# Layers' weighted values in 64x32 tiles of the array: each product of 64 value columns becomes two of 32

## The chip, the cores and the metric

The kernel is one program on one core of a Trainium2 chip. The time is the device time of one execution in microseconds (us). Lower is better.

## The reference, cut to what matters

The model has two blocks over x of shape (4, 512, 128). The first block has a test-time-training layer and then a stack of six transformer layers. The second has an attention with relative positions and a mixture of experts. The change touches only the six layers. Each layer projects x to queries, keys and values of 16 heads of width 64, normalizes and rotates q and k, and attends locally: each window of 32 tokens sees itself and the 32 tokens before it.

```python
DIM, DEPTH, HEADS, DIM_HEAD, WINDOW = 128, 6, 16, 64, 32
def local_attention(q, k, v):              # q, k, v: b h n d
    bq, bk, bv = (t.reshape(b, h, nw, w, d) for t in (q, k, v))
    bk2, bv2 = look(bk), look(bv)          # the window before and the own one: 2*w keys
    sim = jnp.einsum('bhwie,bhwje->bhwij', bq, bk2) * QK_SCALE
    sim = jnp.where(mask, -jnp.finfo(sim.dtype).max, sim)
    attn = jax.nn.softmax(sim, -1)
    out = jnp.einsum('bhwij,bhwje->bhwie', attn, bv2)
    return out.reshape(b, h, n, d)
for i in range(DEPTH):
    x = attn_layer(shift_tokens(x), Wqkv[i], ...) + x
    x = ffn_layer(shift_tokens(x), ln_g[i], ...) + x
```

The last `einsum` is the step that is changed: for each head and window, 32 rows of 64 weights times 64 rows of 64 values.

## The kernel before

All data is float32. The program has four phases that end in a meeting of all engines: test-time training, the transformer layers, the relative attention, the experts. The layers take the stretch from about 188 to 1830 us of the profiled execution.

**Tiling of the layers.** A unit is one layer for one of the 4 batch rows, so there are 24 units, u = 4 * layer + batch. A unit has 4 tiles of 128 tokens, and a tile has two parts (h = 0 and 1, eight heads each): 192 parts in all, counted m. A part goes through: scores (`PE`), a scaling copy and the row maximum (`DVE`), exponentials (`ACT`), reciprocals (`DVE`), scaling (`POOL`), a transpose of the weights (L1216, `PE`), a copy of the transposed weights to `pT` (L1360, `ACT`), the product with the values (L1226, `PE`), and a copy of the result to `oT` (L1365, `ACT`). After the second part of a tile the result goes through the output projection (L1234, `PE`).

**Order.** No planner runs. `rounds()` writes out, once for all engines, a list of (kind, number, step), and each engine runs through it and issues what it has at each step. A part starts every 4 rounds, and `PART_AT` gives its steps: score 0, turn 5, weigh 6, o_copy 8, mix 9. So in the order of TensorE the weighing of one part stands between the scores of later parts, and around both stand the next unit's projections (L1109 to L1111, 512 columns each), the sums of squares (L1139) and the feed-forward network of an earlier unit (L1159 to L1185). TensorE runs everything in that order. It waits by semaphores for what other engines must have ready, for instance `pt_kept` before the weighing.

**The scores, L1208.** Per part a loop over 4 groups, 2 halves, 4 blocks of 32 tokens and 2 heads gives 64 calls of `matmul`. Each uses 32 rows and 32 columns of the array and streams 64 columns. The trace holds 128 weight loads and 128 matmuls for it: a float32 product is two pairs of instructions.

**The weighing, L1226.** Per part a loop over a (2), blk (4), o (2) and f (2) gives 32 calls, 64 pairs of instructions in the trace. f picks the head of a pair, which lies in partitions 64f to 64f + 63 of `pT` and of `v_win`. The 64 value columns are the stationary operand and the 32 tokens of a window the streamed one. The result goes to partitions `to` to `to + 63` of bank 2 + o, with `to` = 64 * ((f + o) % 2), so that four calls in a row use the four 64x64 tiles of the array.

**Buffers around it.** `v_win` is read from the second buffer of two and is filled by DMAs from SP's queue. Before a new one is filled, SP waits for `weighted` of two tiles earlier. ACT's copy to `oT` waits for `weighted` of the same part. The transposes of the next part wait for this copy.

Of the kernel before, what the change touches and what calls it, by code (L numbers as in the profile page):

```python
# [16 lines left out]
P = 128  # L17
# [7 lines left out]
DEPTH, HEADS, DH, WIN = 6, 16, 64, 32  # L25
# [685 lines left out]
GROUPS_TF, HALF_D = 4, DH // 2  # L711
# [167 lines left out]
def ring_take(c, t, *user):  # L879
    k = t.ring[user]  # L880
    if k >= 2:
        c.PE.wait_ge(*ring_freed(t, *t.ring_users[k - 2]))
    return ring_bank(c, t, *user)
# [198 lines left out]
def transformer_tensor(c, t):  # L1082
    PE, psum = c.PE, c.psum
    norm_center(c, t, 0)
    table_tensor(c, t, 0)
    norm_sums(c, t, 0)
    for n in range(1, len(TABLES)):
        table_tensor(c, t, n)
    norm_spread(c, t, 0)
    for b in range(1, B):  # L1090
        norm_center(c, t, b)
    for b in range(1, B):
        norm_sums(c, t, b)
    PE.wait_ge(*t.once.all())
    PE.wait_ge(*t.prepared.on(0))
    PE.wait_ge(*t.tab_kept.all())
    for now in rounds():
        for kind, n, s in now:
            if kind == "spread":
                norm_spread(c, t, n)  # L1100
            elif kind == "part":
                part_tensor(c, t, n, s)
            elif kind == "unit":
                unit_tensor(c, t, n, s)
# [84 lines left out]
def part_tensor(c, t, m, s):  # L1189
    PE, psum, (n, h) = c.PE, c.psum, divmod(m, 2)  # L1190
    u, i = divmod(n, TPB)
    q, k, v = t.q[u % 2], t.k[u % 2], t.v[n % 2]
    if s == PART_AT["score"]:
        PE.wait_ge(*t.k_scaled.on((u, GROUPS_TF - 1)))
        PE.wait_ge(*t.made.on((u, 2 * GROUPS_TF - 1)))
        if m:
            PE.wait_ge(*t.scores_kept.on(m - 1))
        mask = t.maskb[:, 0 if i == 0 else 1, :].unsqueeze(1).to_broadcast([P, GROUPS_TF, 2 * WIN])
        for x in range(2):
            PE.e.matmul(psum[:, x, 0:GROUPS_TF * 2 * WIN].rearrange("p (g k) -> p g k", g=GROUPS_TF), c.identb[:, :], mask, start=True, stop=False)  # L1200
        for g in range(GROUPS_TF):
            for half in range(2):
                for blk in range(TPB):
                    tok, out = i * P + blk * WIN, slice(g * 2 * WIN, (g + 1) * 2 * WIN)
                    for f in range(2):
                        j = 2 * h + f
                        rows = slice(HALF_D * j, HALF_D * (j + 1))
                        last = PE.e.matmul(psum[WIN * blk:WIN * (blk + 1), f, out], q[rows, g, half, tok:tok + WIN], k[rows, g, half, tok:tok + 2 * WIN],  # L1208
                                           start=False, stop=(half == 1 and g == GROUPS_TF - 1))
        last.then_inc(*t.scored.by(m))  # L1210
    if s == PART_AT["turn"]:
        PE.wait_ge(*t.p_scaled.on(m))
        if m:
            PE.wait_ge(*t.o_kept.on(m - 1))
        for g in range(GROUPS_TF):
            last = PE.e.transpose(psum[:, 2, g * P:(g + 1) * P], t.p[h][:, g, :, :].rearrange("p f k -> p (f k)"), c.ident[:, :])  # L1216
        last.then_inc(*t.turned.by(m))
    if s == PART_AT["weigh"]:
        PE.wait_ge(*t.pt_kept.on(m))
        PE.wait_ge(*t.v_in[n % 2].on((n, 9 if i else 7)))  # L1220
        for a in range(2):
            for blk in range(TPB):
                for o in range(2):
                    for f in range(2):
                        rows, to, at = slice(DH * f, DH * f + DH), (f + o) % 2 * DH, a * P + blk * WIN
                        last = PE.e.matmul(psum[to:to + DH, 2 + o, at:at + WIN], v[rows, blk, 2 * (2 * a + o) + h, :],  # L1226
                                           t.pt[h][rows, 2 * a + o, blk * WIN:(blk + 1) * WIN], start=True, stop=True)
        last.then_inc(*t.weighted.by(m))
    if s == PART_AT["mix"] and h == 1:
        PE.wait_ge(*t.o_kept.on(m))  # L1230
        PE.wait_ge(*t.wo_in.on((u // B, 7)))
        ps = ring_take(c, t, "part", m, "mix")
        for e in range(PAIRS):
            last = PE.e.matmul(ps[:, 0:P], t.wo[:, e, :], t.ot[e % 2][:, e // 2, :], start=(e == 0), stop=(e == PAIRS - 1))  # L1234
        last.then_inc(*t.mixed.by(n))
# [1256 lines left out]
```

## Time and profile before

| | us |
|---|---|
| median of 3 runs | 2531.78 |
| lowest and highest | 2521.78, 2538.67 |
| span of the profiled execution | 2515.4 |
| TensorE matmul busy in it | 2362.9 (94%), 53,677 instructions |
| TensorE weight loads busy | 1738.9 (69%), 53,677 instructions |
| VectorE, ScalarE, GpSimd busy | 1744.7, 1598.6, 1463.1 |

Matmuls and weight loads are listed apart, since a load runs beside the matmuls ahead of it. Matmuls are pipelined: the next one starts before the last one has ended, so a group's busy time is the time covered by at least one of its matmuls, and its mean is the length of a single one with its latency. "issue" as a releaser means that the engine waited for nothing that the profile shows, that is, for its own instructions.

### The profile page before, as it was taken

The numbers are of one execution on the slowest core, as the hardware profiler recorded it, in microseconds if no ns is written. First come the engines' busy times: TensorE is split into PE (matmuls) and PEld (weight loads), VectorE is DVE, ScalarE is ACT, GpSimd is POOL, SyncE is SP. The second block draws the span as 40 slices with busy tenths as digits, with TensorE's granted clock in tenths as the row PEclk, the third lists the DMA queues.
The fourth block names the chain that finished last, engine by engine and source line by source line (L and its number), as shares of the span: only waits on it lengthen the run. The fifth ranks groups of instructions, "written<-read, shape, count | busy, mean of one in ns | idle before, by whom it ended". The sixth has DMA issues, their size and how long they took to land.

```text
span 2515.4 us, 122084 instructions
## 1 busy us (share of the span) xinstructions
PE 2362.9 (94%) x53677; PEld 1738.9 (69%) x53677; DVE 1744.7 (69%) x3537; ACT 1598.6 (64%) x5036; POOL 1463.1 (58%) x1408
## 2 busy tenths in 40 slices
PE   9958999999999999999999999999878999999967
PEld 8836777777777777777777777777645666666657
DVE  4477888888878888878787888887335555555534
ACT  3226777777777787777777877777625444545422
POOL 1166667656666667666666677665117656566307
PEclk9979999999999999999999999999979999999978
DMA  4013333333333334333333343333216222222136
GB/s 91 15 33 86 85 78 96 95 80 85 93 88 94 81 83 103 92 83 81 88 95 85 79 97 82 84 92 84 57 22 185 48 48 48 48 48 48 30 95 250
DMA packets 230210, 204.62 MB, mean 81 GB/s; under 512 B 133687, under 2 KB 155464, under 8 KB 229552
## 3 DMA queue, kind: packets, MB, share of 16 engines
q1 hardware_dynamic: 225296, 190.91, 30.6%
q8 instruction: 422, 6.91, 1.2%
q0 software_dynamic: 2208, 5.58, 0.6%
q14 instruction: 108, 0.88, 0.1%
q10 hardware_dynamic: 2176, 0.33, 0.1%
HBM read 86.05 MB, written 15.70 MB: 40 GB/s over the span
## 4 chain that ended last, share of the span: by engine, by line
PE 72%; DVE 17%; issue 4%; SPq 2%; ACT 2%; DMA 1%; POOL 1%; POOLq 0%; ACTq 0%; DVEq 0%
PE psum L1208 8%; PE psum L1226 6%; PE psum L1955 5%; PE psum L1234 5%; PE psum L1109 5%; PE psum L1934 5%; PE psum L1940 4%; PE psum L1111 4%; PE psum L1110 3%; DVE kT L1443 3%; PE psum L1989 3%; PE psum L1979 3%; DVE rotated L1418 3%; PE psum L1185 2%; PE psum L1216 2%
## 5 line engine op out<-in xcount | busy, mean ns | idle before, releaser
L1354 ACT ACTIVATE p<-p,stat 128x64 f32<-128x64 f32 x1536 | 512.5, 336 | 40.1 <-DVE stat L1490 38.0
L1573 POOL TENSOR_TENSOR p<-p,inverse 128x512 f32<-128x512 f32 x192 | 200.2, 1043 | 465.9 <-DVE inverse L1493 464.9
L1208 PE MATMUL psum<-kT,qT 32*32 32x64 f32 x24576 | 306.7, 223 | 30.3 <-issue 29.1
L2088 DVE TENSOR_REDUCE largest<-psum 128x1 f32<-128x512 f32 x256 | 165.0, 686 | 228.0 <-PE psum L1940 228.0
L1208 PEld LDWEIGHTS psum<-kT,qT 32*32 32x32 f32 x24576 | 264.0, 103 | 82.2 <-issue 81.1
L1354 ACT ACTIVATION_READ_ACCUMULATOR p<-p,stat 128x1 f32 x1536 | 288.6, 188 | 0.0
L1418 DVE SCALAR_TENSOR_TENSOR rotated<-psum,scales,rotary 128x512 f32<-128x512 f32 x384 | 271.1, 742 | 24.3 <-ACT sq L1290 24.2
L1552 POOL TENSOR_TENSOR sq<-sq 128x512 f32<-128x512 f32 x192 | 245.1, 1276 | 42.4 <-ACT sq L1290 42.1
L1290 ACT ACTIVATE sq<-psum 128x512 f32<-128x512 f32 x384 | 212.8, 581 | 63.3 <-PE psum L1139 45.9
L1226 PEld LDWEIGHTS psum<-pT,v_win 64*64 64x64 f32 x12288 | 197.3, 135 | 47.6 <-issue 40.6
L1109 PE MATMUL psum<-xs,wqkv_high 128*128 128x512 f32 x384 | 204.9, 534 | 24.3 <-DVE rotated L1418 24.3
L2010 ACT ACTIVATE w_by_key<-psum 128x512 f32<-128x512 f32 x128 | 76.4, 597 | 230.5 <-PE psum L1955 230.5
L1226 PE MATMUL psum<-pT,v_win 64*64 64x32 f32 x12288 | 218.6, 221 | 1.5 <-ACT pT L1360 1.5
L1234 PEld LDWEIGHTS psum<-oT,wo 128*128 128x128 f32 x1536 | 188.0, 196 | 37.0 <-issue 28.0
L1234 PE MATMUL psum<-oT,wo 128*128 128x128 f32 x1536 | 198.9, 283 | 7.5 <-issue 4.2
L1360 ACT ACTIVATE pT<-psum 128x512 f32<-128x512 f32 x192 | 114.3, 596 | 135.7 <-PE psum L1216 135.5
L1303 ACT ACTIVATE v_tok<-psum 128x512 f32<-128x512 f32 x192 | 113.8, 593 | 96.5 <-PE psum L1111 78.7
L2100 POOL TENSOR_TENSOR q_by_head<-q_heads,mask_head 64x256 fp32r<-64x256 f32 x252 | 156.8, 622 | 15.4
L1559 POOL TENSOR_TENSOR qT<-qT,rotated 128x512 f32<-128x512 f32 x96 | 165.7, 1726 | 0.0
L2056 ACT ACTIVATE weights<-psum,largest 128x512 f32<-128x512 f32 x256 | 161.3, 687 | 3.6 <-DVE largest L2088 3.6
L1443 DVE TENSOR_TENSOR kT<-kT,rnorm_wide 128x1024 f32<-128x1024 f32 x96 | 155.7, 1622 | 5.4 <-DMA rnorm_wide<-rnorms 5.3
L1111 PE MATMUL psum<-xs,wqkv_high 128*128 128x512 f32 x384 | 155.0, 404 | 0.0
(352 smaller groups left out, 5448.6 us busy)
## 6 DMA issues: line engine op xcount, KB each, us to landing
v_win<-v_tok SPq DMA_DIRECT2D x576, 128.0 KB
rnorm_wide<-rnorms SPq DMA_DIRECT2D x384, 64.0 KB
v_win<-v_tok SPq DMA_DIRECT2D x336, 64.0 KB
q_rows<-q_rows_all SPq DMA_DIRECT2D x32, 512.0 KB, 4.6
tile_weights<-expert_table SPq DMA_DIRECT2D x23, 512.0 KB, 6.1
wqkv<-L_ffn_Wqkv SPq DMA_DIRECT2D x96, 64.0 KB, 2.4
rel_values<-sq SPq DMA_DIRECT2D x60, 64.0 KB, 2.2
wo<-L_ffn_Wo SPq DMA_DIRECT2D x48, 64.0 KB
```

The source lines that it names most:

```text
L1109: PE.e.matmul(out, w[0], x[1], start=True, stop=False)
L1111: return PE.e.matmul(out, w[0], x[0], start=False, stop=True)
L1208: last = PE.e.matmul(psum[WIN * blk:WIN * (blk + 1), f, out], q[rows, g, half, tok:tok + WIN], k[rows, g, half, tok:tok + 2 * WIN], start= ...
L1226: last = PE.e.matmul(psum[to:to + DH, 2 + o, at:at + WIN], v[rows, blk, 2 * (2 * a + o) + h, :], t.pt[h][rows, 2 * a + o, blk * WIN:(blk + ...
L1234: last = PE.e.matmul(ps[:, 0:P], t.wo[:, e, :], t.ot[e % 2][:, e // 2, :], start=(e == 0), stop=(e == PAIRS - 1))
L1290: A.e.activation(t.sq[half][:, :], c.psum[:, 4 + half, :], ACT.Square).then_inc(*t.squared.by((u, (p, half))))
L1354: last = A.e.activation(p, p, ACT.Exp, bias=t.stat[:, h, 2 * g + f:2 * g + f + 1], accum_out=t.sum[:, h, g, f:f + 1])
L1418: last = V.e.scalar_tensor_tensor(out=rot[x], in0=psum[:, 4 + half, :], scalar=scale, in1=table, op0=ALU.mult, op1=ALU.mult)
L1443: V.e.tensor_tensor(k, k, t.wide[g % 2][:, :].unsqueeze(1).to_broadcast([P, 2, S]), ALU.mult).then_inc(*t.k_scaled.by((u, g)))
L1552: G.e.tensor_tensor(t.sq[0][:, :], t.sq[0][:, :], t.sq[1][:, :], ALU.add).then_inc(*t.squares.by((u, p)))
L1559: G.e.tensor_tensor(second, second, t.turned_by[1][:, :], ALU.add).then_inc(*t.made.by((u, p)))
L1573: G.e.tensor_tensor(p, p, t.inv[:, h, :, :].unsqueeze(3).to_broadcast([P, GROUPS_TF, 2, 2 * WIN]), ALU.mult).then_inc(*t.p_scaled.by(m))
```

## The change

In the weighing of a part the loop over the 64 value columns is split in two halves of 32 (`HALF_D` is 32). A new loop over d = 0 and 32 stands outside the loops over o and f. Each call now loads 64 rows by 32 value columns, writes 32 partitions of the result beginning at `to + d`, and streams the same 32 columns of `pT`. So eight calls in a row use eight tiles of 64x32. The number of calls per part goes from 32 to 64. What is computed, the banks, the semaphores and everything else stay the same.

```diff
         for a in range(2):
             for blk in range(TPB):
-                for o in range(2):
-                    for f in range(2):
-                        rows, to, at = slice(DH * f, DH * f + DH), (f + o) % 2 * DH, a * P + blk * WIN
-                        last = PE.e.matmul(psum[to:to + DH, 2 + o, at:at + WIN], v[rows, blk, 2 * (2 * a + o) + h, :],
-                                           t.pt[h][rows, 2 * a + o, blk * WIN:(blk + 1) * WIN], start=True, stop=True)
+                for d in range(0, DH, HALF_D):
+                    for o in range(2):
+                        for f in range(2):
+                            rows, to, at = slice(DH * f, DH * f + DH), (f + o) % 2 * DH + d, a * P + blk * WIN
+                            last = PE.e.matmul(psum[to:to + HALF_D, 2 + o, at:at + WIN], v[rows, blk, 2 * (2 * a + o) + h, d:d + HALF_D],
+                                               t.pt[h][rows, 2 * a + o, blk * WIN:(blk + 1) * WIN], start=True, stop=True)
         last.then_inc(*t.weighted.by(m))
```

## Rows read from the trace of the kernel before

**Rows 1.** The page: busy time and share of each engine, and the chain.

```profile
PE 2362.9 (94%) x53677; PEld 1738.9 (69%) x53677; DVE 1744.7 (69%) x3537; ACT 1598.6 (64%) x5036; POOL 1463.1 (58%) x1408
...
PE 72%; DVE 17%; issue 4%; SPq 2%; ACT 2%; DMA 1%; POOL 1%; POOLq 0%; ACTq 0%; DVEq 0%
```

**Rows 2.** Windows of 300 us and the layers' whole: busy us (instructions), clock, DMA.

```profile
600.00:900.00 300.00, 291.26 (x7922) 1.00 0.37 90
188.00:1830.00 1642.00, 1583.30 (x43483) 0.99 0.35 86
```

**Rows 3.** Groups by line and form: count, busy us, mean ns, idle before.

```profile
L1208 PE MATMUL psum<-kT,qT 32*32 32x64 f32 x24576 | 306.7, 223 | 30.3 <-issue 29.1
L1226 PE MATMUL psum<-pT,v_win 64*64 64x32 f32 x12288 | 218.6, 221 | 1.5 <-ACT pT L1360 1.5
L1109 PE MATMUL psum<-xs,wqkv_high 128*128 128x512 f32 x384 | 204.9, 534 | 24.3 <-DVE rotated L1418 24.3
...
L1216 PE MATMUL psum<-ident,p 128*128 128x128 f32 x768 | 117.5, 276 | 17.6 <-POOL p L1573 14.5 <-ACT oT L1365 2.6
```

**Rows 4.** The same view for the weight loads.

```profile
L1208 PEld LDWEIGHTS psum<-kT,qT 32*32 32x32 f32 x24576 | 264.0, 103 | 82.2 <-issue 81.1
L1226 PEld LDWEIGHTS psum<-pT,v_win 64*64 64x64 f32 x12288 | 197.3, 135 | 47.6 <-issue 40.6 <-ACT pT L1360 6.9
```

**Rows 5.** Timeline of the matmuls: start us, length us, what, count.

```profile
607.53 0.43 PE L1139 MATMUL psum<-sq,onehot 128*32 128x128 f32 x8
607.88 1.14 PE L1226 MATMUL psum<-pT,v_win 64*64 64x32 f32 x64
608.95 0.50 PE L1109 MATMUL psum<-wqkv_low,xs 128*128 128x512 f32 x1
...
610.77 1.48 PE L1208 MATMUL psum<-kT,qT 32*32 32x64 f32 x128
```

**Rows 6.** Timeline of the loads in the first 0.2 us of a scores' stage.

```profile
627.29 0.29 PEld L1208 LDWEIGHTS psum<-kT,qT 32*32 32x32 f32 x32 [0.21 <-issue]
```

**Rows 7.** The page: the queue that brings TensorE's instructions.

```profile
q8 instruction: 422, 6.91, 1.2%
```

**Rows 8.** Timeline of the loads: two scores' stages that are interrupted.

```profile
616.75 1.22 PEld L1208 LDWEIGHTS psum<-kT,qT 32*32 32x32 f32 x116 [0.21 <-issue]
618.92 0.17 PEld L1208 LDWEIGHTS psum<-kT,qT 32*32 32x32 f32 x12 [0.95 <-issue]
...
650.84 0.94 PEld L1208 LDWEIGHTS psum<-kT,qT 32*32 32x32 f32 x89 [0.21 <-issue]
652.08 0.48 PEld L1208 LDWEIGHTS psum<-kT,qT 32*32 32x32 f32 x39 [0.30 <-issue]
```

**Rows 9.** Windows between such interruptions: us, loads busy (count), clock, DMA.

```profile
618.91:652.07 33.16, 24.92 (x889) 1.00 0.38 101
652.07:686.94 34.87, 24.18 (x889) 1.00 0.34 84
...
704.66:738.88 34.22, 24.12 (x888) 1.00 0.40 89
615.38:618.91 3.53, 2.03 (x137) 1.00 0.29 64
648.98:652.07 3.09, 2.22 (x142) 1.00 0.32 70
```

**Rows 10.** Who waited for whom: us in total, times, longest.

```profile
PEld psum L1208 <- issue: 81.1, 259, 2.0
```

**Rows 11.** The line of the weighing: first and last start.

```profile
L1226 PE MATMUL psum<-pT,v_win x12288: 186/219/313, 197.1 to 1829.4; 64*64 64x32 f32 x199
```

## The prediction

> **What bounds the kernel now.** I read the page first. TensorE's matmuls cover 94% of the span and no other engine more than 69%; in the chain of work that ended last, 72% is TensorE's [rows 1]. Next the windows: in the layers, where the change lies, TensorE is busy for 1583 of 1642 us, and for 291 of 300 us in their middle, at the full granted clock of 2.4 GHz [rows 2]. So time added to TensorE's order in the layers shows almost whole in the end, and time saved there too, unless it falls where TensorE waits for others. There are few such waits: 24.3 us for the rotations, 17.6 us before the transposes, 1.5 us before the weighing [rows 3]. Last I read the groups by line and the timeline, since a busy share does not say what holds the engine. A 94% busy engine may be computing, loading weights, or be short of instructions.
>
> **What the weighing costs now.** 192 parts with 64 pairs (load and matmul) each take 218.6 + 1.5 = 220.1 us, 1.146 us a part [rows 3]; the timeline has 1.14 us for a typical one, with the next stage 1.07 us after its start [rows 5]. A matmul's own length, 0.22 us, is latency that the next ones overlap. So 64 starts lie within 1.14 - 0.22 = 0.92 us, 14.6 ns apart. The matmuls stream only 32 columns, whereas a load of 64 columns lasts 135 ns and one of 32 columns 103 ns [rows 4]. I read this stage as held by its loads: each of four tiles takes its next load only every four pairs.
>
> **What the change does to the array.** Every load has half the columns and eight tiles instead of four take turns. If loads bind, a tile needs less time per load and twice as many tiles work at once, so the array could do twice the pairs in less than the present time. The saving can't be more than the stage has, and it isn't there for the taking: the instructions double, from 128 to 256 a part, 12,288 pairs or 24,576 instructions in all. The question is how fast TensorE gets its instructions.
>
> **The price of a pair in 128 pairs.** The scores are the nearest row: 128 pairs a part, eight tiles in turn. They take 306.7 + 30.3 = 337.0 us, 1.755 us a part [rows 3]. Three facts in them:
> - The first 32 pairs go fast: 32 loads in 0.29 us, less 0.10 us for the length of the last, 31 gaps of 6.1 ns [rows 6]. I take them as instructions that had been queued while the long matmuls ahead ran.
> - A scores' stage without interruption takes 1.48 us in all [rows 5], so (1.48 - 0.22)/127 = 9.9 ns a pair. Beyond the first 32 the pairs come slower, though the array shows at the start that it can take them at 6.1 ns. So in the rest they come at the pace of supply, about 11 ns.
> - Some stages are interrupted by "issue" for 0.3 to 0.95 us [rows 8]. Between two such places there are 889, 889 and 888 loads [rows 9], some 7 x 127. The instruction queue moved 6.91 MB in 422 packets [rows 7]: 16 KB each, and 6.91 MB over 2 x 53,677 instructions is 64 bytes, so a packet is 256 instructions, 128 pairs less a few semaphore instructions. The interruptions stand at multiples of a packet. The packets ahead of two of them lasted 3.53 and 3.09 us [rows 9]. So a packet that is used up in under about 3 to 3.5 us has to wait for the next.
>
> The weighing now runs at 14.6 ns a pair, slower than the supply, and shows no such wait. With 128 pairs at 32 columns it becomes a stage like the scores.
>
> **The sum, on the profiled execution's 2515.4 us.**
> - Lower end of the added time: every weighing costs as an uninterrupted scores' stage: 1.48 - 1.14 = 0.34 us x 192 = 65 us.
> - As an average scores' stage: 1.755 - 1.146 = 0.61 us x 192 = 117 us. Of these, (1.755 - 1.48) x 192 = 53 us are interruptions.
> - Interruptions become more frequent. Parts follow each other every (1829.4 - 197.1)/191 = 8.55 us [rows 11]. The layers hold 43,483/192 = 226 pairs a part [rows 2], 1.77 packets, 4.8 us each. After: 290 pairs, 2.27 packets in about 9.2 us, 4.05 us each, near the 3.1 to 3.5 us at which a packet is late, and now both scores and weighing use one up within 1.5 us. Twice 53 us are at stake (scores and weighing); I take half more, +53 us. The bounds are 0 and twice as much more, +106 us, with a further 30 us for longer waits at each.
> - Taken up by waits of TensorE that exist now (24.3 + 17.6 us [rows 3] and smaller ones): -15 us, between 0 and -40.
>
> Sum: 117 + 53 - 15 = 155 us, so 2670 us for a profiled execution. The median of the runs lies 16 us above the profiled span (2531.78 against 2515.4), so I forecast 2687 us, 6% slower. ACT's copy to `oT` comes 0.3 to 0.6 us later in each part and with it the next transposes; these are two rounds off and TensorE is the one that is late for them, so I add nothing. If the copy had no such room, 192 x 0.3 us would be added, within the range. SP's refill of `v_win`, which waits for the weighing of two tiles earlier, moves by the same fraction of a microsecond in a distance of two tiles (17 us): nothing.
>
> The Trainium skill speaks against the interruptions: its page "Runtime: NRT & Kernel Launch", section "Instruction fetch mechanics", has TensorE's instructions brought in blocks of 16 KB by a queue of their own while earlier ones run, so that crossing a block is mostly hidden. The trace agrees on the block and not on the hiding. By that page alone the sum would be the 65 us of the lower end at most. Its page "TensorE: Matmul & The Clock Gate", in the section "Wait — 56ns, not 53.3ns?", puts the least distance of two matmuls at about 25 ns; by that a stage of 128 pairs would take over 3 us, and the scores' 9.9 ns here rule it out.
>
> **The rivals.**
> - *Supply keeps up, the stage gets shorter (the other sign).* If all 128 pairs came at the 6.1 ns of the first 32, a stage would take 127 x 6.1 ns + 0.22 us = 0.99 us against 1.14: -0.15 x 192 = -28 us, 2504 us. It decides from below (1.14 - 0.22)/127 = 7.2 ns a pair. For it: the loads are smaller than the scores' and the streamed columns are half, so if the 11 ns later in the scores' stage were the array's doing and not the supply's, the weighing would escape it. Against it: the same tiles and forms ran at 6.1 ns just before. Chance 0.05.
> - *No change.* The stage gets to about 7.2 ns a pair, or waits elsewhere in the layers take up all: they are some 40 us against 65 at least. 2531 us. Chance 0.05.
> - *Supply floor alone.* Packets come in time, as for scores without interruption: 65 - 15 = 50 us, 2582 us. For it: many scores' stages have no interruption, 259 waits for issue in all against 192 that each stage has at its start [rows 10]. Against it: the packets of the weighing come on top. Chance 0.16.
> - *The supply of packets becomes the bound.* Every scores' and weighing stage waits for its packet. 117 + 106 + 30 = 253 us and more, 2785 us. It decides when a packet takes 4 us or more, since the 2.27 packets a part then fill the part's whole time. Chance 0.12.
> - *As forecast*, interruptions in both stages, 2600 to 2770 us. Chance 0.62.
>
> **Range and chances.** The range 2580 to 2785 holds the forecast and the better part of its two neighbours. Measurements of this kernel tell a difference from about 1%. Slower by over 1%: 0.90 (the last three cases); within 1%: 0.05; faster by over 1%: 0.05.
>
> **What would show it.** In the profile after: TensorE has 53,677 + 12,288 = 65,965 matmuls; the instruction queue some 96 packets more (24,576/256); the weighing's line shows 24,576 matmuls of form 64*32, with loads near 103 ns. If the forecast is right, a weighing stage has 1.4 us or more in the timeline with 128 pairs, its group gets idle time by "issue", the busy time and idle time of L1226 together go from 220 to 340 us or more, and the scores' line, which isn't touched, also gains idle time by issue over its 30.3 us. If the supply floor alone holds, the scores' line stays at 337 us. If the rival with the other sign is right, the weighing's stage is 1.0 us long and without issue waits. I am wrong on the cause if the stage is longer with evenly spaced pairs from the very first, since then the array and not the supply limits a 64x32 tile.

## The result, and the profile after

| | before | after |
|---|---|---|
| median | 2531.4 us (4 runs) | 2809.84 us (4 runs) |
| span of the profiled execution | 2515.4 us | 2803.6 us |
| mean granted clock over the span | 0.971 | 0.938 |

The changed kernel is 11% slower: the ratio is 1.110, with a 95% interval of 1.107 to 1.114. The profiled spans differ by 288 us. The forecast was 155 us more for the profiled execution and 2687 us for the median, with 2785 us as the upper end of the range.

The page of the changed kernel answers [rows 1] and [rows 7]:

```profile
PE 2502.6 (89%) x65965; PEld 1841.9 (66%) x65965; DVE 1741.3 (62%) x3537; ACT 1603.8 (57%) x5036; POOL 1432.5 (51%) x1408
...
q8 instruction: 518, 8.49, 1.3%
...
PE 86%; issue 8%; DVE 2%; POOL 1%; DMA 1%; ACT 1%; another core or an unknown queue 0%; ACTq 0%; POOLq 0%; SPq 0%; DVEq 0%
```

TensorE has the 12,288 matmuls more that were expected, and its instruction queue the 96 packets more. Yet TensorE is busy for only 89% instead of 94% of a longer span, and in the chain "issue", time without any other releaser, goes from 4% to 8%. So TensorE is more on the path that sets the end, and stands idle more. The groups by line (out<-in, form, count | busy us, mean ns of one | idle us before, releaser) answer [rows 3] and [rows 4]. L1227 is the weighing, L1235 the output projection:

```profile
L1208 PE MATMUL psum<-kT,qT 32*32 32x64 f32 x24576 | 330.9, 229 | 107.4 <-issue 106.4
L1227 PE MATMUL psum<-pT,v_win 64*32 64x32 f32 x24576 | 262.8, 201 | 58.9 <-issue 57.2 <-ACT pT L1361 1.4
L1235 PE MATMUL psum<-oT,wo 128*128 128x128 f32 x1536 | 234.0, 314 | 19.2 <-issue 18.4 <-ACT oT L1366 0.7
...
L1208 PEld LDWEIGHTS psum<-kT,qT 32*32 32x32 f32 x24576 | 273.0, 106 | 169.3 <-issue 168.2
L1227 PEld LDWEIGHTS psum<-pT,v_win 64*32 64x32 f32 x24576 | 234.2, 105 | 112.9 <-issue 104.4 <-ACT pT L1361 7.4
```

Busy and idle time of each line, added up:

| line | before | after | difference |
|---|---|---|---|
| weighing | 220.1 | 321.7 | +101.6 us |
| scores (not touched) | 337.0 | 438.3 | +101.3 us |
| output projection (not touched; 198.9 + 7.5 before) | 206.4 | 253.2 | +46.8 us |
| the rest of 288.2 | | | +38.5 us |

Only about a third of the loss lies in the line that was changed. Of the last row, 15.5 us lie behind the layers, in phases that the change doesn't touch: from the last start of the weighing to the end of the span it is 686.0 us before (2515.4 less 1829.4 [rows 11]) and 701.5 us after (2803.6 less 2102.1). In the traces of the experiments below it takes between 680 us (with half of the change) and 700 us (with kernels that have none of it), so these 15.5 us can't be put down to the change. The layers themselves lost 273 us. The timeline of TensorE in one stretch shows how the loss comes about (start us, length us, what, count, idle before):

```profile
682.40 1.22 PE L1227 MATMUL psum<-pT,v_win 64*32 64x32 f32 x120
685.51 0.33 PE L1227 MATMUL psum<-pT,v_win 64*32 64x32 f32 x8 [1.89 <-issue]
...
687.80 2.05 PE L1208 MATMUL psum<-kT,qT 32*32 32x64 f32 x128
...
691.65 3.62 PE L1235 MATMUL psum<-oT,wo 128*128 128x128 f32 x16
...
697.64 1.29 PE L1227 MATMUL psum<-pT,v_win 64*32 64x32 f32 x128
```

And the windows around it (us; busy us and count of PE, PEld, DVE, ACT, POOL; granted clock, DMA share, GB/s):

```profile
683.50:685.00 1.50, 0.12 (x14) 0.01 (x1) 1.33 (x6) 1.49 (x8) 0.00 (x0) 1.00 0.00 0
685.00:695.20 10.20, 9.69 (x160) 7.40 (x160) 5.03 (x12) 2.17 (x4) 4.80 (x4) 0.50 0.43 106
695.20:700.00 4.80, 4.80 (x157) 3.97 (x156) 3.64 (x17) 3.87 (x19) 0.65 (x1) 1.00 0.37 83
```

The weighing stops after 120 of its 128 matmuls for 1.89 us. Then the granted clock is 0.50 (the lower level, 1.2 GHz) for 10.2 us, in which the scores take 2.05 us without any interruption (1.48 us in [rows 5]) and the output projection 3.62 us. A weighing without interruption takes 1.29 us. Its loads in the first 0.2 us:

```profile
697.64 0.26 PEld L1227 LDWEIGHTS psum<-pT,v_win 64*32 64x32 f32 x33 [0.20 <-issue]
```

The first 33 pairs come (0.26 - 0.10)/32 = 5 ns apart, against 8.6 ns over the whole stage. So the pairs are not evenly spaced from the very first, which the prediction had named as the sign that the array and not the supply limits a 64x32 tile.

The trace's record of the transfers on TensorE's instruction queue ties the waits to the packets. In the layers of the changed kernel, TensorE's matmuls waited for issue 192 times for more than 0.3 us, and each of these waits ends 2.2 to 3.0 us after the start of the latest packet's transfer. The closest two packets start 3.26 us apart, and on average one starts every 4.4 us.

### The profile page after: what moved, and what is told of

It is laid out like the page before. It is cut to its first block, busy times and chain, and to the rows that moved or that the text cites. A ratio compares the mean times of both kernels' runs of the same rounds, so it can differ in the third digit from the quotient of the medians.

```text
span 2803.6 us, 146660 instructions
## 1 busy us (share of the span) xinstructions
PE 2502.6 (89%) x65965; PEld 1841.9 (66%) x65965; DVE 1741.3 (62%) x3537; ACT 1603.8 (57%) x5036; POOL 1432.5 (51%) x1408
## 4 chain that ended last, share of the span: by engine, by line
PE 86%; issue 8%; DVE 2%; POOL 1%; DMA 1%; ACT 1%; another core or an unknown queue 0%; ACTq 0%; POOLq 0%; SPq 0%; DVEq 0%
PE psum L1208 11%; PE psum L1227 9%; PE psum L1235 8%; PE psum L1109 7%; PE psum L1111 5%; PE psum L1110 5%; PE psum L1956 5%; PE psum L1935 4%; PE psum L1216 3%; PE psum L1941 3%; PE psum L1177 3%; PE psum L1990 2%; PE psum L1139 2%; PE psum L1180 2%; PE psum L1980 2%
## 5 line engine op out<-in xcount | busy, mean ns | idle before, releaser
L1208 PE MATMUL psum<-kT,qT 32*32 32x64 f32 x24576 | 330.9, 229 | 107.4 <-issue 106.4
L1208 PEld LDWEIGHTS psum<-kT,qT 32*32 32x32 f32 x24576 | 273.0, 106 | 169.3 <-issue 168.2
L1227 PE MATMUL psum<-pT,v_win 64*32 64x32 f32 x24576 | 262.8, 201 | 58.9 <-issue 57.2
L1227 PEld LDWEIGHTS psum<-pT,v_win 64*32 64x32 f32 x24576 | 234.2, 105 | 112.9 <-issue 104.4
L1235 PEld LDWEIGHTS psum<-oT,wo 128*128 128x128 f32 x1536 | 223.5, 226 | 58.5 <-issue 53.4
L1235 PE MATMUL psum<-oT,wo 128*128 128x128 f32 x1536 | 234.0, 314 | 19.2 <-issue 18.4
L1109 PE MATMUL psum<-xs,wqkv_high 128*128 128x512 f32 x384 | 207.9, 541 | 24.0 <-DVE rotated L1419 24.0
L1486 DVE TENSOR_TENSOR p<-psum,rnorm_tok 128x512 f32<-128x512 f32 x192 | 131.7, 686 | 62.3 <-PE psum L1208 54.2
L1419 DVE SCALAR_TENSOR_TENSOR kT<-psum,scales,rotary 128x512 f32<-128x512 f32 x192 | 142.9, 744 | 43.9 <-PE psum L1208 25.4
L1559 POOL TENSOR_TENSOR kT<-kT,rotated 128x512 f32<-128x512 f32 x96 | 122.8, 1279 | 71.4 <-DVE kT L1419 70.9
```

The source lines that it names most:

```text
L1109: PE.e.matmul(out, w[0], x[1], start=True, stop=False)
L1227: last = PE.e.matmul(psum[to:to + HALF_D, 2 + o, at:at + WIN], v[rows, blk, 2 * (2 * a + o) + h, d:d + HALF_D], t.pt[h][rows, 2 * a + o, b ...
L1419: last = V.e.scalar_tensor_tensor(out=rot[x], in0=psum[:, 4 + half, :], scalar=scale, in1=table, op0=ALU.mult, op1=ALU.mult)
```

## The experiments

Two theories stood against each other in the expectations. *Supply*: TensorE gets its instructions in packets of 256; a packet used up too early leaves it waiting, and these waits are the loss. *Tile*: the 64x32 form is slow by itself. Beside them stood the clock, as a cost of its own or not.

**The new tiles without more instructions**

```diff
-                for d in range(0, DH, HALF_D):
+                for d in (range(0, DH, HALF_D) if m == 0 else (blk % 2 * HALF_D,)):
```

> The weighing uses 64x32 tiles as in the changed kernel, but only one of the two halves of 32 value columns is computed (the lower in even blocks of 32 tokens, the upper in odd ones; the first part has both): 64 pairs of instructions a part, as many as before, and half of the values is left out. Supply theory (the time goes where TensorE waits for packets of 256 instructions): the new form costs nothing by itself; the weighing takes under 0.8 us a part, the scores' line stays near its 337 us busy and idle, and the whole is 2460 to 2500 us, faster than before. Tile theory (64x32 tiles or their changes of mode are slow by themselves): the weighing's pairs cost as in the changed kernel (307 us / 24,576 = 12.5 ns) and what it does to the scores (some 100 us more) stays, so 2570 to 2600 us.

2514.1 us against 2530.33, ratio 0.994 (0.989 to 0.999). The lines by form of this kernel:

```profile
L1208 PE MATMUL psum<-kT,qT 32*32 32x64 f32 x24576 | 308.9, 223 | 45.7 <-issue 45.0
L1227 PE MATMUL psum<-pT,v_win 64*32 64x32 f32 x12352 | 148.4, 200 | 3.6 <-issue 2.0 <-ACT pT L1361 1.6
```

The form isn't slow: 64 pairs cost 152.0/192 = 0.79 us a part, against 1.146 us in 64x64 tiles. That speaks against the tile theory. But the whole became faster by 16 us, far less than the 68 us that the line lost, and the 2460 to 2500 us that the supply theory had given were missed. The scores took back 18 us (354.6 against 337.0, where the expectation had them unchanged). A likely reason, which no run isolates, is that the parts follow each other faster and the packets with them. In the waits of TensorE, those for ACT's copy to `oT` and for the softmax's scaling are now 8.1 and 24.3 us (3.2 and 14.5 before).

**The old tiles with as many instructions**

```diff
+def tiny_products(c, n, bank):
+    for k in range(n):
+        to = k % 4 * HALF_D
+        c.PE.e.matmul(c.psum[to:to + HALF_D, bank, k:k + 1], c.ident[:, 0:HALF_D], c.ident[:, 0:1], start=True, stop=True)
...
         PE.wait_ge(*t.v_in[n % 2].on((n, 9 if i else 7)))
+        tiny_products(c, 32, 3)
         for a in range(2):
```

> The kernel before with its 64x64 tiles, and ahead of each weighing 32 products of one streamed column (128 rows, 32 columns of the array), whose results are overwritten: the instruction count of the changed kernel in other forms. Supply theory: the scores, which are not touched, lose as in the changed kernel (their line goes from 337 to 420 us and more, with the growth in idle time by issue), the output projection too, and the whole is 2740 to 2810 us. Tile theory: the additional pairs cost only themselves, 64 x 6 to 8 ns x 192 = 75 to 100 us, so 2605 to 2630 us, and the scores stay at 337 us.

2784.03 us, ratio 1.099 (1.095 to 1.103). Its lines:

```profile
L1215 PE MATMUL psum<-kT,qT 32*32 32x64 f32 x24576 | 322.7, 228 | 60.4 <-issue 58.9
L1234 PE MATMUL psum<-pT,v_win 64*64 64x32 f32 x12288 | 231.5, 221 | 36.9 <-issue 36.9
...
L1193 PE MATMUL psum<-ident 128*32 128x1 f32 x12288 | 145.7, 172 | 2.3 <-ACT pT L1368 1.4 <-issue 0.5
```

The whole is within 1% of the changed kernel, without one 64x32 tile in the weighing. It lies in the range of the supply theory partly by luck: the tiny products themselves cost 148 us, where I had worked out 75 to 100 us. The rest stands in lines that were not touched, 124 us together: scores +46 us (383.1), weighing +48 us (268.4), output projection +30 us (217.0 + 19.2 = 236.2). This is the part that shows what more instructions do to their neighbours. The scores' loss is half of what the changed kernel has, so that part of the expectation was missed.

**The same additional instructions, spread**

```diff
+        tiny_products(c, 16, 4 + at)
         three_products(PE, psum[:, 4 + at, :], w, xs).then_inc(*t.projected.by((u, (p, at))))
```

> The same number of tiny products, but 16 ahead of each of the 16 projections of a unit instead of 32 ahead of each weighing: as many instructions per part, away from the dense stages. If only the density in a burst mattered (scores and weighing back to back), the scores would stay near 337 us and the whole near 2531 + 75 to 100 us = 2605 to 2630 us. If the number of packets in the time matters as well, since each has to be used up later than some 3.4 us after the last, the scores still lose 40 to 80 us and the whole is 2680 to 2760 us, below the run with the same products at the weighing.

2757.04 us, ratio 1.089 (1.085 to 1.092).

```profile
L1216 PE MATMUL psum<-kT,qT 32*32 32x64 f32 x24576 | 309.9, 224 | 55.2 <-issue 54.2
L1234 PE MATMUL psum<-pT,v_win 64*64 64x32 f32 x12288 | 220.4, 221 | 2.1 <-ACT pT L1368 1.5 <-issue 0.4
L1194 PE MATMUL psum<-ident 128*32 128x1 f32 x12288 | 175.2, 174 | 24.3 <-DVE rotated L1426 16.7 <-issue 7.1
```

Here the products take 199.5 us with the waits for `rotated` that now fall on them. The harm to others is smaller: scores +28 us, weighing +2 us. So where the instructions stand matters. The total is in the expected range, but the scores' loss is below the 40 to 80 us that I had given. The total is only 27 us lower than with the products at the weighing, because 384 short stages cost more by themselves than 192.

**Nothing but instructions.** Behind the kernel's last work:

```diff
+            for k in range(2048):
+                rows, to = slice(DH * (k % 2), DH * (k % 2) + DH), k // 2 % 4 * HALF_D
+                c.PE.e.matmul(c.psum[to:to + HALF_D, k % 2, 0:1], c.ident[rows, 0:HALF_D], c.ident[rows, 0:1], start=True, stop=True)
```

> The kernel before, and behind its last work a stream of 2048 products of one column in 64x32 tiles: 4096 pairs, 8192 instructions, 32 packets, with nothing else running. Supply theory: a packet comes every 3.4 to 3.9 us whatever is in it, so 27 to 30 ns a pair, 109 to 125 us for the stream. If the supply were what the uninterrupted scores' stage shows (9.9 ns a pair), 41 us; if it kept the pace of the first 32 pairs (6.1 ns), 25 us.

2644.12 us, 114 us more; this kernel was timed once. Timeline of the loads, and a window over 29 such groups:

```profile
2533.25 1.26 PEld L158 LDWEIGHTS psum<-ident 64*32 64x32 f32 x128 [2.02 <-issue]
2536.72 1.26 PEld L158 LDWEIGHTS psum<-ident 64*32 64x32 f32 x128 [2.21 <-issue]
2540.19 1.26 PEld L158 LDWEIGHTS psum<-ident 64*32 64x32 f32 x128 [2.21 <-issue]
...
2533.20:2638.30 105.10, 36.67 (x3712) 0.50 0.02 5
```

This shows the supply by itself. TensorE takes just 128 pairs in 1.26 us and then has nothing for 2.0 to 2.8 us, again and again: 105.1/29 = 3.62 us for each packet of 256 instructions. The DMA share is 0.02, so the packet's time isn't contention with other transfers. The granted clock is 0.50 in this window, but the 3.3 us between the closest packets of the layers, where the clock is mostly 1.00, is about the same as here (3.33 us), so the supply's pace isn't an effect of the lower clock. Within a packet the pairs come (1.26 - 0.10)/127 = 9.1 ns apart.

**The change where the scores are short, and its base.** Both kernels take half of the scores' products:

```diff
-            for half in range(2):
+            for half in range(1):
...
-                                           start=False, stop=(half == 1 and g == GROUPS_TF - 1))
+                                           start=False, stop=(g == GROUPS_TF - 1))
```

> The kernel before with half of the products of the scores: only the first 32 of each head's 64 dimensions are multiplied, so the scores are not complete, and a part has 32 products there (64 pairs) instead of 64. It is the base for the next run. Supply theory: without a stage of 128 pairs hardly any stage waits for a packet; the scores' line falls from 337 us to 130 to 170 us, idle time by issue near 0, and the whole is 2330 to 2370 us.

> The changed kernel with the same halved scores: the layers' instruction count of the kernel before, the dense stage of 128 pairs now at the weighing. Supply theory: the harm of the change depends on what stands beside it, so here it costs only 90 to 150 us over the other run with halved scores (2440 to 2500 us) instead of the 278 us that it costs in full; the weighing's line keeps 230 us and more busy with 20 to 50 us idle by issue, the scores stay short. Tile theory (the 64x32 form has its price by itself): the same 278 us on top, 2610 to 2650 us.

Base: 2506.41 us, ratio 0.992 (0.989 to 0.995). With the change: 2535.19 us, ratio 1.003 (1.001 to 1.005). So here the change costs 29 us, not 278, and also far less than the 90 to 150 us of the supply theory's expectation. First the lines of the base, then the lines of the other:

```profile
L1234 PE MATMUL psum<-oT,wo 128*128 128x128 f32 x1536 | 203.1, 287 | 47.9 <-ACT oT L1365 45.5
L1216 PE MATMUL psum<-ident,p 128*128 128x128 f32 x768 | 122.2, 283 | 61.1 <-POOL p L1573 47.5 <-ACT oT L1365 12.4
...
L1226 PE MATMUL psum<-pT,v_win 64*64 64x32 f32 x12288 | 219.6, 221 | 2.6 <-ACT pT L1360 1.9
L1208 PE MATMUL psum<-kT,qT 32*32 32x64 f32 x12288 | 165.1, 223 | 0.0
```

```profile
L1227 PE MATMUL psum<-pT,v_win 64*32 64x32 f32 x24576 | 267.3, 201 | 40.2 <-issue 37.1 <-ACT pT L1361 1.9
L1208 PE MATMUL psum<-kT,qT 32*32 32x64 f32 x12288 | 181.6, 223 | 49.3 <-issue 49.0
...
L1235 PE MATMUL psum<-oT,wo 128*128 128x128 f32 x1536 | 199.6, 284 | 16.4 <-ACT oT L1366 13.9 <-issue 2.1
L1216 PE MATMUL psum<-ident,p 128*128 128x128 f32 x768 | 117.2, 275 | 13.3 <-POOL p L1574 10.9 <-ACT oT L1366 2.2
```

I was wrong on the base by 136 us and more: 172 us less in the scores made the kernel only 22 us faster. TensorE now waits for the softmax (47.5 us) and for the copy to `oT` (45.5 us). So another chain ends nearly as late as TensorE's work, and what is taken from TensorE brings little.

The same waits make the 29 us too small as a price of the change. Its weighing loses 85 us (222.2 to 307.5, with 40 us idle), for 102 us in the full kernel. The scores, which were to stay short, lose 66 us (165.1 to 230.9) for 101 us there. Together that is some 50 us less harm. The output projection, which lost 47 us there, waits for issue for only 2.1 us here, and the mean granted clock is no lower with the change (0.966 against 0.961 over the profiled spans). On the other side, waits of the base were filled: the line of the output projection is 35 us and that of the transposes 53 us shorter than in the base. So the lines shown put some 100 us of the difference between 278 and 29 us down to harm that didn't occur, and some 80 us to room that the base has; the rest isn't settled. A fixed price of 278 us, as the tile theory has it, would leave some 200 us even with that room. The price depends on what stands beside the change, as supply says.

**Half of the change.** The 32-column form only in parts with h = 0:

```diff
-                for d in range(0, DH, HALF_D):
+                wide = DH if h else HALF_D
+                for d in range(0, DH, wide):
...
-                            last = PE.e.matmul(psum[to:to + HALF_D, 2 + o, at:at + WIN], v[rows, blk, 2 * (2 * a + o) + h, d:d + HALF_D],
+                            last = PE.e.matmul(psum[to:to + wide, 2 + o, at:at + WIN], v[rows, blk, 2 * (2 * a + o) + h, d:d + wide],
```

> The change in every second part only (h = 0 as in the changed kernel, h = 1 with 64x64 tiles as before): 2.02 packets of 256 instructions a part instead of 2.27 or 1.77. A price per changed part (tile form) gives just half of the 278 us, 2665 to 2675 us. Supply theory with a threshold (a packet hurts only when used up in under some 3.4 us): it rises faster at the end than at the start, so the first half of the change costs less than the second: 90 to 130 us, 2620 to 2660 us.

2609.77 us against 2518.07 beside it, ratio 1.037 (1.034 to 1.040). Half of the change costs 3.7%, a third of the 11% of the whole. A fixed price per changed part would give 5.5%. The lines tell where the difference arises:

```profile
L1208 PE MATMUL psum<-kT,qT 32*32 32x64 f32 x24576 | 315.7, 224 | 54.9 <-issue 54.1
L1228 PE MATMUL psum<-pT,v_win 64*32 64x32 f32 x12288 | 136.4, 201 | 27.6 <-issue 26.6 <-ACT pT L1362 0.7
L1228 PE MATMUL psum<-pT,v_win 64*64 64x32 f32 x6144 | 111.1, 222 | 0.7 <-ACT pT L1362 0.7
```

The weighing itself loses 56 us (275.8 against 220.1), about half of the 102 us of the full change. The scores lose only 34 us (370.6) of 101 us. So it is the harm to the neighbours that grows faster at the end, as a threshold has it.

**The scores in two pieces**, a long group of matmuls between them, before and after the change (`rest_tensor` issues the second piece and is called behind each of the long groups):

```diff
...
+        scores(range(GROUPS_TF // 2))
+        t.rest = lambda: scores(range(GROUPS_TF // 2, GROUPS_TF)).then_inc(*t.scored.by(m))
```

> The kernel before, complete, with the scores of a part issued in two pieces of 64 pairs and the next long group of matmuls (a projection, an output projection or a part of the feed-forward network) between them. Supply theory: each piece is mostly in TensorE's queue when it begins and packets are used up more evenly: the scores' line loses 30 to 80 us of its 337 us, and the whole is 2460 to 2510 us if the later scores don't make TensorE wait for the softmax. If instead the order only shifts work, the time stays within 1% of 2531 us; if the delay of the scores hits the transposes, more than 20 us are added.

> The changed kernel with the scores in two pieces in the same way, the weighing in one. Supply theory: as many packets a part (2.27), but spread better, so 2700 to 2770 us against 2810 us, with less idle time by issue in the scores' line than the 107 us of the changed kernel. Tile theory: no difference from 2810 us beyond 1%.

Before with two pieces: 2586.4 us, ratio 1.023 (1.021 to 1.026), slower instead of faster. After with two pieces: 2807.48 us, ratio 1.111 (1.107 to 1.115), no difference from the changed kernel, which is what the tile theory had said; the supply theory had said 2700 to 2770 us. Line, timeline and two waits of the first:

```profile
L1225 PE MATMUL psum<-kT,qT 32*32 32x64 f32 x24576 | 331.4, 222 | 0.2
...
646.74 0.85 PE L1225 MATMUL psum<-kT,qT 32*32 32x64 f32 x64
648.42 0.85 PE L1225 MATMUL psum<-kT,qT 32*32 32x64 f32 x64
...
PE psum L1255 <- ACT oT L1387: 24.5, 50, 1.6
PE psum L1149 <- DVE z L1519: 22.5, 21, 1.1
```

The interruptions did go: 30.3 us of idle time before, 0.2 now. But two pieces take 2 x 0.85 = 1.70 us, one undisturbed stage 1.48, and the later scores make TensorE wait for the copy and for the sum in z. So supply can be smoothed by order, and it didn't pay. After the change the scores' line still has 59.1 us idle by issue (106.4 in the changed kernel). Between the two kernels with pieces the change costs 221 us (2807.48 less 2586.4), not 278, so the smoother order does soften the change, by about as much as the pieces themselves cost. Why these two cancel so closely isn't settled, and by its total this run doesn't speak for supply.

**More work for the array per instruction**

```diff
+                if a == 1 and blk % 2 == 0:
+                    PE.e.matmul(psum[:, 3, 256:512]..., c.identb[:, :], t.maskb[:, 1, :]..., start=True, stop=True)
```

> The changed kernel with two pairs more in each weighing: a bf16 matmul of 128x128 by 256 columns that keeps the array busy for about 0.11 us each and whose result nobody reads. It asks whether the fall of the granted clock (TensorE is at the lower of its two levels for some 200 us of the layers, against some 20 us before) is a cost of its own that more array work per instruction takes back. If so, the time at the lower level falls to 100 us or less, the output projection's line (234 us, 199 us before) falls towards 210 us, and the total rises by less than the 2 x 0.11 x 192 = 42 us that the matmuls take. If the clock only follows the waits, nothing of it changes and the total rises by 40 to 90 us.

2786.78 us against 2518.07 beside it, ratio 1.107 (1.104 to 1.111), where the changed kernel has 1.110 (1.107 to 1.114): the 384 additional matmuls cost nothing that can be measured. Its output projection, its filling matmuls, and the windows of the layers for this kernel:

```profile
L1237 PE MATMUL psum<-oT,wo 128*128 128x128 f32 x1536 | 220.1, 302 | 13.4 <-issue 12.5 <-ACT oT L1368 0.8
L1224 PE MATMUL psum<-maskb,identb 128*128 128x256 bf16 x384 | 109.0, 284 | 1.1 <-issue 1.1
...
190.00:2100.00 1910.00, 1764.08 (x55959) 1276.58 (x55942) 1289.21 (x2640) 1260.16 (x4371) 1019.11 (x814) 0.97 0.30 75
```

and for the changed kernel:

```profile
190.00:2100.00 1910.00, 1713.39 (x55532) 1271.43 (x55530) 1294.80 (x2640) 1254.77 (x4381) 1017.10 (x814) 0.95 0.30 75
```

A mean granted clock of 0.95 over 1910 us means some 190 us at the lower level (2 x 0.05 x 1910), 0.97 some 115 us, and 0.99 before [rows 2] some 33 us. The means are rounded; the stretches at the lower level that the traces record in the layers add up to 208 us, 130 us and 20 us. So the time at the lower level fell, but not to the 100 us or less that I had expected. The output projection gave back 20 of its 47 us.

That the lower level costs time is shown: the same output projection takes 3.62 us at it. Why the clock comes back here is not shown. The filling also gives the queue time, and TensorE waits less for issue (84.8 + 32.5 + 12.5 us in scores, weighing and output projection, where the changed kernel has 106.4 + 57.2 + 18.4). The changed kernel's own trace ties the clock to these waits: in the layers it falls 46 times, and at 44 of these places a wait for issue of more than 1 us is under way or has ended less than 3 us before. There are 78 such waits, so not each of them brings a fall.

## Why the prediction was wrong

- **What bounds the kernel: half right.** TensorE sets the end, and added time counts almost whole. The sentence that saved time would show too was wrong: in two runs 68 and 172 us less in a line brought 16 and 22 us. It did no harm to this forecast, as nothing was saved.
- **The array: right.** The 64x32 tiles do 64 pairs in 0.79 us instead of 1.146.
- **The price of an uninterrupted stage: too high.** I took the scores' 1.48 us; it is 1.29 us. So this term is (1.29 - 1.14) x 192 = 29 us, not 65 us. The pairs come 8.6 ns apart (1.29 less 0.20 us of latency, over 127) in place of 9.9.
- **The weighing as a whole: right within 15%, by luck.** It lost 101.6 us for the forecast 117, since more interruptions made up for the shorter stage. With its share of the next term, I had expected the line at 340 us or more; it has 321.7.
- **"Interruptions become more frequent": the step that failed.** I gave it 53 us, and at most 106 and 30 more; with the 53 us in the term before it, that makes 106 us of waits. The waits for issue in the layers' lines grew by 155 us (106.4 + 57.2 + 18.4 + 6.3, against 29.1 + 4.2). The untouched scores alone lost 101 us and the output projection, which the term left out, 47 us. I had worked out the mean use of a packet after the change, 4.05 us, against the 3.1 to 3.5 us of [rows 9], and read the difference as room. But the mean isn't what decides. The parts came (2102.1 - 197.3)/191 = 9.97 us apart, 4.4 us a packet, more than the 3.62 us of the stream, and the waits were there all the same. The mean is over packets with the long matmuls too; a dense stage of 128 pairs uses one packet up in 1.3 us, so a packet that holds one can end too early, now twice a part. TensorE waited for issue 129 times in the scores (106.4 us) and 54 times in the weighing (57.2 us), against 53 times (29.1 us) in the scores and never in the weighing before.
- **The rival *the supply of packets becomes the bound*** had the direction and, with 2785 us and more, a time that fits, with a chance of 0.12 from me. Its conditions were not met: a packet takes 3.62 us and not 4 us or more, and at most 183 of the 384 stages waited (129 + 54 waits), not every one. That its time fits is in part luck, as it has neither the output projection nor the clock in it.
- **A term that was missing: the clock.** In the layers its mean went from 0.99 to 0.95, with the falls at long waits for packets, and then large matmuls take nearly twice as long: the output projection 3.62 us, where one in the kernel before, at 636.67 us with the clock at 1.00, took 1.95 us. An upper bound is half of the 188 us more at the lower level (208 less 20), 94 us, if all of it were work bound by the array. The runs don't isolate its share.
- **Taken up by other waits: about right in size.** The transposes' wait for the softmax's scaling fell from 14.5 to 4.4 us, for -15 us in the sum.
- **The terms as the runs have them,** an estimate: 155 us of waits for issue, 29 us for the longer stage, -10 us taken up, and at its upper bound 94 us by the clock. Together that is at most 268 us, where the layers lost 273 us.
- **The other sign and no change: excluded,** as the pace of the first 32 pairs doesn't last over a packet.
- **A slip without effect:** two tiles are four parts, so SP's refill has 34 us (4 x 8.55) and not 17 us.

The Trainium skill's page "Runtime: NRT & Kernel Launch", section "Instruction fetch mechanics", has the crossing of a 16 KB block as mostly hidden. The measurement decides otherwise: the stream waits for more than 2 us of each 3.62 us, and the changed kernel's scores for 106.4 us in all. The block's size agrees with the 128 pairs of each group.

## What to carry to other kernels

Count TensorE's instructions, and not only their work. Where short matmuls stand densely, look for "issue" waits whose distance is a multiple of 128 pairs, and compare how long each packet of 256 instructions lasts (not their mean) with the 3.3 to 3.6 us that one took here. Splitting a product for more parallel tiles doubled its instructions here; the loss showed mostly in the neighbours' lines, and in the granted clock. When one engine is the bound at 94%, check with a run that leaves work out whether another chain ends just behind it, before counting on a gain.

## What the runs showed of the hardware

- A packet of 256 instructions reaches TensorE every 3.62 us on average (105.1 us for 29), with a DMA share of 0.02; in its transfers and in those of the layers the closest two packets start 3.3 us apart.
- In the changed kernel's layers each of the 192 waits for issue of more than 0.3 us ends 2.2 to 3.0 us after the latest packet's transfer began.
- The pace inside a packet is 9.1 ns a pair in the stream (at a clock of 0.50), 8.6 ns in the weighing and 9.9 ns in the scores. The first 32 pairs of a stage come 6.1 ns apart in the scores [rows 6] and 5 ns in the weighing.
- After a wait of 1.89 us for instructions in the middle of tiny matmuls the granted clock was 0.50 for 10.2 us. In the stream of tiny pairs, busy for 36.67 of 105.10 us, it was 0.50 throughout. Of the 46 falls in the changed kernel's layers, 44 stand at a wait for issue of more than 1 us.
- The 64x32 tiles took 64 pairs in 0.79 us, where 64x64 tiles, with twice the value columns in each pair, took 1.146 us.
